# Down products of fourteen experts as two 64-row halves in two banks each, in a cross-attention and mixture-of-experts kernel

## The chip, the core and the metric

The kernel runs on one core of one Trainium2 chip. The metric is the device time of one execution in microseconds (us). Engines are called PE (TensorE; PEld is its weight load), ACT (ScalarE), DVE (VectorE), POOL (GpSimd) and SP (SyncE).

## What is computed

The reference normalizes x (8 sequences of 512 tokens, 256 wide), adds a cross-attention with 16 heads and sigmoid scores over 1601 context rows, normalizes again, and adds a feed-forward part: one shared expert over all 4096 tokens, and 16 routed experts. Every expert takes the 64 tokens of each sequence with its highest scores (8 x 64 = 512 rows) and adds its weighted output to their rows:

```python
g = einsum('becd,efd->becf', x_tok, Wg)
u = einsum('becd,efd->becf', x_tok, Wu)
h = gelu(g) * u                                  # 512 rows x 512 per expert
eo = einsum('becf,edf->becd', h, Wd) * topk_w    # the down product, 512 rows x 256
flat = flat.at[flat_idx].add(eo.reshape(-1, d))
```

## The kernel before, in words

**Numbers.** Every operand of a large product is split in two parts, hi (rounded to the fp32r format) and lo (the rest), and a product is three: hi x hi, lo x hi and hi x lo (`PRODUCTS`), summed in PSUM.

**The attention part**, up to about 893 us of the profile, works in row halves in most places: PE multiplies rows 0 to 63 and rows 64 to 127 of an operand by two matmuls that follow each other, each into a bank of its own (`ROW_TILES`, lines 1566 to 1619), and DVE adds the two banks when it reads them. The scores (line 1751) use 48 rows in each half. The weighted sum (line 1780) uses 128 rows with 32 columns of the array for each of four matmuls. The first tasks (`BEFORE`, lines 1669 and 1682, and `out_product`, line 1634, for the last sequence) do the same products with whole 128-row matmuls.

**The expert part** is a loop over 24 units: the shared expert on the 8 sequences (n = 0 to 7), then the 16 experts (n = 8 to 23, e = n - 8, so n = 9 is the second expert). A unit has four quarters of the hidden width: PE makes the gate and the up product of a quarter (`up`, line 1839, 6 matmuls of 128 x 128 by 512 columns for each), ACT takes the gelu of the gate (`gelus`, line 891), DVE multiplies it by the up product (`hidden_products`, line 1321), ACT writes the hi part of the result (`hidden_hi`, line 899) and DVE the lo part (`hidden_lo`, line 1328). PE's order in `expert(e)` is written out by hand: quarters 0 and 1 of unit n, the down product of unit n - 1, quarters 2 and 3 of unit n. The last unit, n = 23, is cut finer and has a down product of its own (`last_down`).

**The down product** (`down`, line 1857) makes four tiles of 128 rows x 256. Each is 3 products x 4 quarters = 12 matmuls with 128 x 128 weights (the hidden rows) and 256 moving columns (the down weights). Tiles 0 and 1 lie in the one bank of `d_bank` (the third `score` pair), tiles 2 and 3 in the other; `d_full` counts the filled banks. The banks `acc` and `misc` are used for transposed tokens of the first two experts and for the last unit's tiles, and are idle between.

**After it** ACT scales each tile by the token weights into `result` (`expert_result`, line 944), which it may start when DVE has written `add_w` (`expert_rows`, line 1364), and counts `scaled` after every second tile. POOL waits for `scaled` and adds the rows to the output in HBM by indirect DMA (`add_rows`, line 814). PE waits for `scaled` before it writes a bank again. DVE's order in `expert(e)` is: hidden quarters 0 and 1 of unit n, the next expert's tokens (line 1402 to 1404), a transpose (line 1392), the lo part of the next gate and up weights (line 1341), `expert_rows(e - 1)`, hidden quarters 2 and 3 (lines 1321 and 1328), the lo part of the next down weights. ACT's order is: gelus and hi parts of quarters 0 and 1, the hi part of the next gate and up weights, `expert_result(e - 1)`, quarters 2 and 3.

Of the kernel before, what the change touches and what calls it, by code (L numbers as in the profile page):

```python
# [10 lines left out]
ACT = mybir.ActivationFunctionType  # L11
AX_X = mybir.AxisListType.X

P = 128
B, S, D = 8, 512, 256
# [4 lines left out]
TT = S // P  # L20
# [28 lines left out]
FT = F // P  # L49
SETS = E + 1  # L50
UNITS = B + E
# [5 lines left out]
def key_rows(st):  # L57

    return min(P, T - P * st)
# [166 lines left out]
    return i % FT, slice(S // 2 * (i // FT), S // 2 * (i // FT + 1))  # L226


def wait_past(engine, sem, value):

    if value > 0:
        engine.wait_ge(sem, value)


def build(nc, x, ctx_t, w_attn, gate_t, w_gu, w_d, out):


    with ExitStack() as keep:
        def sem(name):
            return keep.enter_context(nc.semaphore(name))  # L240
# [59 lines left out]
        add_w = [sb(f"add_w{p}", [P, TT]) for p in range(2)]  # L300
# [26 lines left out]
        with ExitStack() as stage_b:  # L327
# [16 lines left out]
            d_hi = [d_hi0, sb("d_hi1", [P, FT, D], F32R)]  # L344
            d_lo = [d_lo0, sb("d_lo1", [P, FT, D], F32R)]
# [3 lines left out]
            hid_hi = [sb(f"hid_hi{i}", [P, FT, S], F32R) for i in range(2)]  # L349
            hid_lo = [sb(f"hid_lo{i}", [P, FT, S], F32R) for i in range(2)]  # L350
            result = [sb(f"result{i}", [P, TT, D]) for i in range(2)]
# [11 lines left out]
        acc = keep.enter_context(nc.psum_tensor("acc", [P, S], F32))  # L363
        misc = keep.enter_context(nc.psum_tensor("misc", [P, S], F32))
# [14 lines left out]

        g_bank, u_bank, d_bank, t_bank = score[0], score[1], score[2], [acc, misc]  # L380

        last_bank = [d_bank[:, 0, 0:D], d_bank[:, 1, 0:D], acc[:, 0:D], misc[:, 0:D]]


# [45 lines left out]
        resid_read = [sem(f"resid_read{i}") for i in range(2)]  # L430
        g_full = sem("g_full")
        u_full = sem("u_full")
        gelu_done = sem("gelu_done")
        hidden_done = sem("hidden_done")
        hid_hi_done = sem("hid_hi_done")
# [3 lines left out]
        scaled = sem("scaled")  # L439
# [18 lines left out]
        PRODUCTS = ((0, 0), (0, 1), (1, 0))  # L458
# [369 lines left out]
        def _(act):  # L828
# [11 lines left out]
            for t in range(2):  # L840
                last = act.activation(xn[:, t, :], xn[:, t, :], ACT.Identity, bias=rs_mean[:, t:t + 1],
                                      scale=rs[:, t:t + 1])
# [24 lines left out]
            for n in range(QUADS):  # L867
                rows = key_rows(n % NST)
# [66 lines left out]
            def expert_result(e, par, tiles=range(TT)):  # L935
                act.wait_ge(adds_ready, 2 * e + 1)
                for t in tiles:
                    if e + 1 == E:
                        act.wait_ge(d_full, 2 * (e + B) + t + 1)
                        act.activation(result[par][:, t, :], last_bank[t], ACT.Copy, scale=add_w[par][:, t:t + 1]  # L940
                                       ).then_inc(scaled, 1)
                        continue
                    act.wait_ge(d_full, 2 * (e + B) + t // 2 + 1)
                    last = act.activation(result[par][:, t, :], d_bank[:, t // 2, D * (t % 2):D * (t % 2 + 1)],  # L944
                                          ACT.Copy, scale=add_w[par][:, t:t + 1])
                    if t % 2:
                        last.then_inc(scaled, 1)
# [25 lines left out]
        def _(dve):  # L973
# [236 lines left out]
            def copy_out(task):  # L1210
# [21 lines left out]
                if kind in "KV" and LAST_OF[b, task[3] if kind == "K" else task[2]] == task:  # L1232
# [6 lines left out]
                    elif kc == 2 and b + 1 < B:  # L1239
# [22 lines left out]
                                     op0=ALU.mult, op1=ALU.mult).then_inc(ln_first, 1)  # L1262
            for t in range(2, TT):
                last = dve.tensor_scalar(xn[:, t, :], xn[:, t, :], mv[:, t, 0:1], rs[:, t:t + 1],
                                         ALU.subtract, ALU.mult)
# [42 lines left out]
            def hidden_products(n, quarters):  # L1308
                for f in quarters:
                    now = FT * n + f + 1  # L1310
                    _, cols = piece(n, f)
                    of = u_bank[:, f % 2, cols]
                    if n == 0 and f < UPS_EARLY:
                        dve.wait_ge(misc_copied, COUNT["U", B - 1, 1, f])
                        of = early_up[:, 1, S * f:S * (f + 1)]
                    else:
                        dve.wait_ge(u_full, full_of(n) + f + 1)
                    dve.wait_ge(gelu_done, now)
                    wait_past(dve, hid_split, now - 2)

                    dve.tensor_tensor(hidden[:, f % 2, cols], gelu[:, f % 2, cols], of,  # L1321
                                      ALU.mult).then_inc(hidden_done, 1)

            def hidden_lo(n, par, quarters):
                for f in quarters:
                    dve.wait_ge(hid_hi_done, FT * n + f + 1)
                    of, cols = piece(n, f)
                    dve.tensor_tensor(hid_lo[par][:, of, cols], hidden[:, f % 2, cols],
                                      hid_hi[par][:, of, cols].bitcast(F32), ALU.subtract
                                      ).then_inc(hid_split, 1)  # L1330

            def hidden_quarters(n, par, quarters):
                hidden_products(n, quarters)
                hidden_lo(n, par, quarters)
# [24 lines left out]
            def expert_rows(e, par):  # L1359

                dve.wait_ge(shared_out[par], SHARED_OUT)
                for t in range(TT):
                    wait_past(dve, added[t], 16 * (e - 1))
                dve.tensor_copy(add_w[par][:], slot_w[:, :, e]  # L1364
                                ).then_inc(adds_ready, 1)
                dve.tensor_copy(add_row[par][:], slot_row[:, :, e]
                                ).then_inc(adds_ready, 1)

            def rows_of(e, par, before):

                if before:

                    dve.wait_ge(rows_in[par], 8 * TT * (e - par))
                dve.tensor_copy(gather_row[par][:], slot_row[:, :, e]  # L1374
                                ).then_inc(rows_ready, 1)
# [11 lines left out]
            def turn(e):  # L1387

                par = e % 2
                dve.wait_ge(rows_in[par], 8 * TT * (e - par) + 16 * TT)  # L1390
                wait_past(dve, placed, PLACE_DMAS * (e - DIRECT_ROWS))
                dve.transpose(blocks.rearrange("p j (t q) -> p t j q", q=TURN),
                              gathered[par][:].rearrange("p t (j q) -> p t j q", q=TURN)).then_inc(turned, 1)
# [102 lines left out]
            for n in range(2, B):  # L1496
                par = n % 2
# [28 lines left out]
            def expert(e, par):  # L1526
                n = e + B
                hidden_quarters(n, par, (0, 1))
                if e + 1 < DIRECT_ROWS:
                    tokens(1 - par)  # L1530
                    rows_of(e + 3, 1 - par, True)
                elif e + 1 < E:
                    turned_tokens(e + 1)
                if e + 2 < E:
                    turn(e + 2)
                if e + 4 < E:
                    rows_of(e + 4, par, True)
                if e + 1 < E:
                    set_lo(0, par, e + 2)
                if e == 0:  # L1540
                    shared_result(B - 1)
                else:
                    expert_rows(e - 1, 1 - par)
                hidden_quarters(n, par, (2, 3))
                if e + 1 < E:
                    set_lo(1, par, e + 2)
# [9 lines left out]
        def _(pe):  # L1556
            ROW_TILES = [slice(ROWS * e, ROWS * (e + 1)) for e in range(2)]
# [288 lines left out]
            def down(n, par, slot):  # L1846

                pe.wait_ge(hid_split, FT * (n + 1))
                for t2 in range(2):
                    if n <= B:  # L1850
                        wait_past(pe, d_copied, 2 * n + t2 - 1)
                    else:
                        pe.wait_ge(scaled, 2 * (n - B) + t2 - 1)
                    for t in range(2 * t2, 2 * t2 + 2):
                        for j, (a, b) in enumerate(PRODUCTS):
                            for f in range(FT):
                                mm = pe.matmul(d_bank[:, t2, D * (t % 2):D * (t % 2 + 1)],  # L1857
                                               (hid_hi, hid_lo)[a][par][:, f, P * t:P * (t + 1)],
                                               (d_hi, d_lo)[b][slot][:, f, :],
                                               start=(j == 0 and f == 0), stop=(j == 2 and f == FT - 1))  # L1860
                    mm.then_inc(d_full, 1)
# [35 lines left out]
            for n in range(2, B):  # L1897
                par = n % 2
# [4 lines left out]
                if n == 4:  # L1903
                    pe.wait_ge(soft_step, SOFT_DONE)
                    for t in range(TT):
                        mm = pe.transpose(t_bank[0][:, P * t:P * (t + 1)],
                                          logits[:, t, :, :].rearrange("p b e -> p (b e)"), ident[:])
                    mm.then_inc(tok_full, tf.up())
                down(n - 1, 1 - par, 0)
                if n == 2:  # L1910
                    pe.wait_ge(gates_in, 16 * TT * B)
                    for t in range(TT):
                        mm = pe.transpose(t_bank[0][:, P * t:P * (t + 1)], logits_t[:, P * t:P * (t + 1)], ident[:])
# [75 lines left out]
```

## Time and profile before

| | us |
|---|---|
| median of 3 runs (lowest, highest) | 1309.55 (1308.88, 1310.62) |
| the profiled execution | 1305.85 |
| its span | 1304.0 |
| PE busy, share of the span | 98% |
| DVE, ACT, POOL busy | 56%, 76%, 22% |

The profile is of one execution. Its chain is the work that ended last, followed back step by step to what released it. The timeline lists instructions in order of time: start in us, us, engine, line, operation, output<-inputs, for PE the rows x columns of the weights and of the moving operand, and the number of merged instructions. Matmuls overlap each other, so the cost of one is read from start to start, and the second number of a row includes the tail that overlaps the next row. In brackets stands the idle time before the instruction and what ended it.

### The profile page before, as it was taken

The page shows a single profiled execution, that of the slowest core. Times are in us where ns is not written, and L with a number is a line of the kernel's source. Part 1 is how long each engine was busy: PE and PEld are TensorE (multiplying, and loading weights), DVE is VectorE, ACT ScalarE, POOL GpSimd, SP SyncE. Part 2 cuts the span into 40 slices and gives each one's busy share as a digit, 9 for nine tenths or more (in the row PEclk, how much of TensorE's full clock was granted, in tenths as well). Part 3 has the DMA queues.
Part 4 walks back from the last instruction along what each step waited for, and adds up shares of the span by engine and source line. Part 5 has one row for each costly group of instructions (what it writes and reads, how often), then busy time and mean ns, then how long its engine had stood idle before and what let it go on. Part 6 is the DMA issues. An engine that isn't in the chain of part 4 may idle for free.

```text
span 1304.0 us, 25503 instructions
## 1 busy us (share of the span) xinstructions
PE 1283.8 (98%) x10200; PEld 772.1 (59%) x10200; DVE 732.5 (56%) x1377; ACT 985.3 (76%) x1148; POOL 286.9 (22%) x288
## 2 busy tenths in 40 slices
PE   8999999999999999999999999999999999999997
PEld 6445444444454544544444443336888888888887
DVE  6564475365266448437536633215558777777773
ACT  5888989998998899899999989996333455555553
POOL 3000030020002003002000200500001567677635
PEclk9999999999999999999999999999999999999999
DMA  7785973874776597387477549713543577777754
GB/s 215 179 188 126 139 184 111 125 162 133 130 139 166 118 137 171 113 131 148 149 129 140 127 93 156 169 34 114 195 130 110 181 201 192 188 192 190 192 109 49
DMA packets 118726, 190.82 MB, mean 146 GB/s; under 512 B 22448, under 2 KB 71600, under 8 KB 118608
## 3 DMA queue, kind: packets, MB, share of 16 engines
q1 hardware_dynamic: 98768, 155.21, 51.9%
q0 software_dynamic: 19648, 33.72, 12.4%
q8 instruction: 81, 1.33, 0.5%
q10 hardware_dynamic: 192, 0.26, 0.1%
q14 instruction: 37, 0.30, 0.1%
HBM read 108.43 MB, written 55.61 MB: 126 GB/s over the span
## 4 chain that ended last, share of the span: by engine, by line
PE 87%; issue 5%; DMA 2%; DVE 2%; ACT 2%; POOL 1%; SPq 0%; POOLq 0%; DVEq 0%; ACTq 0%
PE score L1839 19%; PE score L1751 18%; PE acc L1780 14%; PE misc L1780 13%; PE score L1857 9%; PE score L1566 5%; PE score L1580 5%; PE score L1589 2%; ACT probs L876 1%; PE score L1619 1%; PE score L1607 1%; DMA key_scr<-key_parts 1%; POOL norm L765 1%; DMA norm<-norm_blocks 1%; DMA ctx_raw<-ctx_t 1%
## 5 line engine op out<-in xcount | busy, mean ns | idle before, releaser
L876 ACT ACTIVATE probs<-score 128x1024 f32<-128x1024 f32 (+1 forms) x832 | 789.8, 1026 | 77.3 <-PE score L1751 70.6
L1751 PE MATMUL score<-queries,keys 48*128 48x512 f32 (+1 forms) x1664 | 312.2, 438 | 6.5 <-ACT probs L876 4.2
L1751 PEld LDWEIGHTS score<-queries,keys 48*128 48x128 f32 (+1 forms) x1664 | 139.1, 180 | 275.0 <-ACT probs L876 212.7
L1780 PE MATMUL acc<-probs,values 128*32 128x512 f32 (+1 forms) x1664 | 210.5, 601 | 0.0
L1780 PE MATMUL misc<-probs,values 128*32 128x512 f32 (+1 forms) x1664 | 205.8, 600 | 0.0
L1026 DVE TENSOR_REDUCE whole<-score 128x512 f32<-128x1024 f32 (+1 forms) x75 | 77.0, 1026 | 196.6 <-PE score L1566 119.6
L729 POOL DMA_DIRECT2D ctx_raw<-ctx_t x32 | 23.4, 733 | 642.6 <-DVE ctx_lo L1004 557.9
L801 POOL DMA_INDIRECT gathered<-norm_scr,gather_row x64 | 81.2, 1269 | 227.5 <-DVE gather_row L1374 212.2
L891 ACT ACTIVATE gelu<-score 128x512 f32<-128x512 f32 (+1 forms) x97 | 55.5, 580 | 84.6 <-PE score L1839 84.0
L814 POOL DMA_INDIRECT out<-result,add_row x64 | 106.6, 1666 | 48.4 <-ACT result L944 25.9
L1839 PE MATMUL score<-tok_hi,gu_hi 128*128 128x512 f32 (+1 forms) x388 | 117.0, 383 | 0.0
L1839 PE MATMUL score<-tok_lo,gu_hi 128*128 128x512 f32 (+1 forms) x388 | 116.2, 381 | 0.0
L1839 PE MATMUL score<-tok_hi,gu_lo 128*128 128x512 f32 (+1 forms) x388 | 116.2, 381 | 0.0
L1321 DVE TENSOR_TENSOR hidden<-gelu,score 128x512 f32<-128x512 f32 (+1 forms) x97 | 64.0, 664 | 92.6 <-PE score L1839 62.3
L899 ACT ACTIVATE hid_hi<-hidden 128x512 fp32r<-128x512 f32 (+1 forms) x100 | 61.0, 613 | 63.9 <-DVE hidden L1321 60.7
L1066 DVE TENSOR_REDUCE values<-score 128x512 f32<-128x1024 f32 (+1 forms) x52 | 59.3, 1141 | 71.7 <-PE score L1580 71.0
L1780 PEld LDWEIGHTS misc<-probs,values 128*32 128x32 f32 (+1 forms) x1664 | 40.7, 108 | 87.0 <-issue 76.6
L1780 PEld LDWEIGHTS acc<-probs,values 128*32 128x32 f32 (+1 forms) x1664 | 38.8, 108 | 77.0 <-issue 71.5
L1839 PEld LDWEIGHTS score<-tok_lo,gu_hi 128*128 128x128 f32 x388 | 71.8, 188 | 14.2
L1839 PEld LDWEIGHTS score<-tok_hi,gu_lo 128*128 128x128 f32 x388 | 71.8, 188 | 14.1
L1839 PEld LDWEIGHTS score<-tok_hi,gu_hi 128*128 128x128 f32 x388 | 70.2, 189 | 12.9 <-issue 0.8
L944 ACT ACTIVATE result<-score,add_w 128x256 f32<-128x256 f32 x60 | 23.6, 474 | 67.9 <-DVE add_w L1364 64.7
(257 smaller groups left out, 1626.2 us busy)
## 6 DMA issues: line engine op xcount, KB each, us to landing
keys<-key_scr SPq DMA_DIRECT2D x180, 200.2 KB, 8.0
key_scr<-key_parts SPq DMA_DIRECT2D x45, 512.0 KB, 8.3
gu_raw<-w_gu SPq DMA_DIRECT2D x17, 1024.0 KB
ctx_raw<-ctx_t POOLq DMA_DIRECT2D x24, 512.0 KB, 5.1
queries<-query_parts SPq DMA_DIRECT2D x186, 64.0 KB, 2.5
d_raw<-w_d SPq DMA_DIRECT2D x17, 512.0 KB
norm<-xn SPq DMA_DIRECT2D x224, 32.0 KB
xn<-x SPq DMA_DIRECT2D x8, 512.0 KB, 3.8
```

The lines of the kernel that those rows point to most:

```text
L801: pool.indirect_dma_start(gathered[par][:, t, :], None, norm_scr[:, :], bass.IndirectOffsetOnAxis(ap=gather_row[par][:, t:t + 1], axis=0)) ...
L814: pool.indirect_dma_start(out[:, :], bass.IndirectOffsetOnAxis(ap=add_row[par][:, t:t + 1], axis=0), result[par][:, t, :], None, compute_o ...
L876: act.activation(probs[0:rows, (n + 1) % RING, 2 * pair:2 * pair + 2, :], score[SLOT[k]][0:rows, :, :], ACT.Sigmoid, scale=SCALE).then_inc ...
L899: act.activation(hid_hi[par][:, of, cols], hidden[:, f % 2, cols], ACT.Copy).then_inc(hid_hi_done, 1)
L1026: dve.tensor_reduce(whole[:, 0:n], score[SLOT[task]][:, :, 0:n].rearrange("p e s -> p s e"), AX_X, ALU.add).then_inc(halves_added, 1)
L1321: dve.tensor_tensor(hidden[:, f % 2, cols], gelu[:, f % 2, cols], of, ALU.mult).then_inc(hidden_done, 1)
L1566: mm = pe.matmul(bank[:, e, 0:n], W2[a][rows, WK, k, P * half:P * (half + 1)], parts_of_ctx(b, kc)[c][rows, k, 0:n], start=(j == 0 and k = ...
L1580: mm = pe.matmul(bank[0:n, e, D * i:D * (i + 1)], parts_of_ctx(b, kc)[a][rows, k, s0:s0 + n], W2[c][rows, WV, k, :], start=(j == 0 and k = ...
L1751: mm = pe.matmul(score[SLOT[k]][0:rows, g, :], keys[quarter % KEY_RING][of, pair, P * st:P * st + rows], queries[half][of, e, pair, :], st ...
L1780: mm = pe.matmul(sums_bank[n // NST % 2][32 * c:32 * (c + 1), :], values[b % 2][0:rows, st, half, c, :], probs[0:rows, (n + 1) % RING, c, ...
L1839: mm = pe.matmul(bank[:, f % 2, cols], (gu_hi, gu_lo)[a][slot][:, w, k, P * of:P * (of + 1)], (tok_hi, tok_lo)[b][par][:, k, cols], start= ...
L1857: mm = pe.matmul(d_bank[:, t2, D * (t % 2):D * (t % 2 + 1)], (hid_hi, hid_lo)[a][par][:, f, P * t:P * (t + 1)], (d_hi, d_lo)[b][slot][:, f ...
```

## The change

For the units with 8 < n < 23 (the second to the fifteenth expert) the down product is cut into two: rows 0 to 63 and rows 64 to 127 of every quarter of the hidden width are multiplied by separate matmuls, which alternate, into two banks: tiles 0 and 1 into the two banks of `d_bank`, tiles 2 and 3 into `acc` and `misc`. ACT scales the first half into `result` and counts the new semaphore `half_scaled`; DVE waits for that, multiplies the other half by the same weights and adds it to `result`, and counts `scaled` after every second tile. DVE does this between `expert_rows` and hidden quarters 2 and 3. The first expert, the shared expert and the last unit stay as they were.

```diff
@@ -224,6 +224,12 @@
     if n + 1 < UNITS:
         return i, slice(0, S)
     return i % FT, slice(S // 2 * (i // FT), S // 2 * (i // FT + 1))
+
+
+def in_halves(n):
+
+
+    return B < n < UNITS - 1
 
 
 def wait_past(engine, sem, value):
@@ -378,6 +384,8 @@
                         o_lo[:]]
 
         g_bank, u_bank, d_bank, t_bank = score[0], score[1], score[2], [acc, misc]
+
+        down_halves = [[d_bank[:, 0, :], d_bank[:, 1, :]], [acc[:], misc[:]]]
 
         last_bank = [d_bank[:, 0, 0:D], d_bank[:, 1, 0:D], acc[:, 0:D], misc[:, 0:D]]
 
@@ -430,6 +438,7 @@
         resid_read = [sem(f"resid_read{i}") for i in range(2)]
         g_full = sem("g_full")
         u_full = sem("u_full")
+        half_scaled = sem("half_scaled")
         gelu_done = sem("gelu_done")
         hidden_done = sem("hidden_done")
         hid_hi_done = sem("hid_hi_done")
@@ -941,6 +950,10 @@
                                        ).then_inc(scaled, 1)
                         continue
                     act.wait_ge(d_full, 2 * (e + B) + t // 2 + 1)
+                    if in_halves(e + B):
+                        act.activation(result[par][:, t, :], down_halves[t // 2][0][:, D * (t % 2):D * (t % 2 + 1)],
+                                       ACT.Copy, scale=add_w[par][:, t:t + 1]).then_inc(half_scaled, 1)
+                        continue
                     last = act.activation(result[par][:, t, :], d_bank[:, t // 2, D * (t % 2):D * (t % 2 + 1)],
                                           ACT.Copy, scale=add_w[par][:, t:t + 1])
                     if t % 2:
@@ -1366,6 +1379,16 @@
                 dve.tensor_copy(add_row[par][:], slot_row[:, :, e]
                                 ).then_inc(adds_ready, 1)
 
+            def other_halves(e, par):
+
+                for t in range(TT):
+                    dve.wait_ge(half_scaled, TT * (e - 1) + t + 1)
+                    last = dve.scalar_tensor_tensor(
+                        out=result[par][:, t, :], in0=down_halves[t // 2][1][:, D * (t % 2):D * (t % 2 + 1)],
+                        scalar=add_w[par][:, t:t + 1], in1=result[par][:, t, :], op0=ALU.mult, op1=ALU.add)
+                    if t % 2:
+                        last.then_inc(scaled, 1)
+
             def rows_of(e, par, before):
 
                 if before:
@@ -1541,6 +1564,8 @@
                     shared_result(B - 1)
                 else:
                     expert_rows(e - 1, 1 - par)
+                    if in_halves(n - 1):
+                        other_halves(e - 1, 1 - par)
                 hidden_quarters(n, par, (2, 3))
                 if e + 1 < E:
                     set_lo(1, par, e + 2)
@@ -1852,7 +1877,14 @@
                     else:
                         pe.wait_ge(scaled, 2 * (n - B) + t2 - 1)
                     for t in range(2 * t2, 2 * t2 + 2):
-                        for j, (a, b) in enumerate(PRODUCTS):
+                        for j, (a, b) in enumerate(PRODUCTS if in_halves(n) else ()):
+                            for f in range(FT):
+                                for e, rows in enumerate(ROW_TILES):
+                                    mm = pe.matmul(down_halves[t2][e][:, D * (t % 2):D * (t % 2 + 1)],
+                                                   (hid_hi, hid_lo)[a][par][rows, f, P * t:P * (t + 1)],
+                                                   (d_hi, d_lo)[b][slot][rows, f, :],
+                                                   start=(j == 0 and f == 0), stop=(j == 2 and f == FT - 1))
+                        for j, (a, b) in enumerate(() if in_halves(n) else PRODUCTS):
                             for f in range(FT):
                                 mm = pe.matmul(d_bank[:, t2, D * (t % 2):D * (t % 2 + 1)],
                                                (hid_hi, hid_lo)[a][par][:, f, P * t:P * (t + 1)],
```

## Rows read from the trace of the kernel before

**Rows 1.** page, its first line:

```profile
span 1304.0 us, 25503 instructions
```

**Rows 2.** the chain of waits in order of time: start us, us, what:

```profile
1062.75 5.75 PE score L1857 x48
...
1085.16 10.91 PE score L1839 x48
...
1276.76 5.76 PE score L1857 x48
```

**Rows 3.** windows: stretch, us, busy by engine (instructions), PEclk, DMA share, GB/s:

```profile
1100.00:1268.00 168.00, 168.00 (x974) 149.07 (x973) 123.17 (x180) 88.55 (x140) 108.75 (x72) 1.00 0.77 180
```

**Rows 4.** timeline of PE, blocks of whole and of half matmuls, and what follows them:

```profile
15.08 0.40 PE L1682 MATMUL score<-w_lo,ctx_hi 128*128 128x256 f32 x2
...
17.59 0.62 PE L1669 MATMUL misc<-ctx_hi,w_hi 128*128 128x512 f32 x2
...
366.33 0.40 PE L1607 MATMUL score<-w_hi,o_hi 64*128 64x256 f32 x4
...
367.75 0.63 PE L1751 MATMUL score<-queries,keys 48*128 48x512 f32 x4
...
378.15 0.39 PE L1580 MATMUL score<-w_hi,ctx_lo 64*128 64x256 f32 x4
...
379.06 0.88 PE L1751 MATMUL score<-queries,keys 48*128 48x512 f32 x4
...
896.37 0.40 PE L1634 MATMUL misc<-w_hi,o_hi 128*128 128x256 f32 x2
...
897.80 0.63 PE L1839 MATMUL score<-tok_hi,gu_hi 128*128 128x512 f32 x2
```

**Rows 5.** timeline of PE, first step from 128-row matmuls to row halves:

```profile
24.18 0.63 PE L1669 MATMUL misc<-ctx_next,w_lo 128*128 128x512 f32 x2
24.74 0.74 PE L1751 MATMUL score<-queries,keys 48*128 48x512 f32 x4
25.31 0.64 PE L1566 MATMUL score<-ctx_hi,w_hi 64*128 64x512 f32 x4
```

**Rows 6.** timeline of PE, row halves, 128 x 32 matmuls, row halves:

```profile
36.28 0.40 PE L1751 MATMUL score<-queries,keys 48*128 48x512 f32 x2
36.61 1.06 PE L1780 MATMUL acc<-probs,values 128*32 128x512 f32 x8
37.61 0.74 PE L1751 MATMUL score<-queries,keys 48*128 48x512 f32 x4
38.17 0.64 PE L1566 MATMUL score<-ctx_hi,w_hi 64*128 64x512 f32 x4
38.63 0.65 PE L1566 MATMUL score<-ctx_lo,w_hi 64*128 64x512 f32 x4
...
41.82 1.92 PE L1780 MATMUL acc<-probs,values 128*32 128x512 f32 x16
43.67 0.72 PE L1751 MATMUL score<-queries,keys 48*128 48x512 f32 x4
```

**Rows 7.** timeline of DVE and ACT behind the down product that ends at 1085.16:

```profile
1086.98 0.16 DVE L1364 COPY add_w<-slot_w 128x4 f32<-128x4 f32 x1
...
1087.17 1.57 ACT L944 ACTIVATE result<-score,add_w 128x256 f32<-128x256 f32 x4 [4.57 <-DVE add_w L1364]
...
1089.32 0.69 DVE L1321 TENSOR_TENSOR hidden<-gelu,score 128x512 f32<-128x512 f32 x1 [2.10 <-issue]
1090.67 0.69 DVE L1321 TENSOR_TENSOR hidden<-gelu,score 128x512 f32<-128x512 f32 x1 [0.66 <-PE score L1839]
1091.27 1.50 DVE L1328 TENSOR_TENSOR hid_lo<-hidden,hid_hi 128x512 fp32r<-128x512 f32 x2
```

**Rows 8.** groups of instructions by form: xcount, busy us, mean ns, idle before:

```profile
L1135 DVE SCALAR_TENSOR_TENSOR o_sum<-misc,mine,o_sum 128x512 f32<-128x512 f32 x16 | 12.0, 749 | 32.6 <-PE misc L1780 32.6
...
L1173 DVE TENSOR_TENSOR nt_lo<-score,nt_hi 128x256 fp32r<-128x256 f32 x28 | 10.6, 420 | 0.5
```

## The prediction, made before the changed kernel had run

> **What bounds the kernel now.** I read the page first, for the span [rows 1], then the chain of waits in order of time over the part that the change touches. The first of the fourteen changed down products starts there at 1062.75 us and the last at 1276.76 us; between them the chain is PE alone, and it repeats: a down product of 48 matmuls takes 5.75 us, and the 48 matmuls of the gate and up products behind it take 10.91 us, with nothing between them [rows 2]. One expert is 16.66 us long. The windows view says the same from the other side: in 168 us of this stretch PE is busy for 168.00, at a granted clock of 1.00 (the 2.4 GHz level), while VectorE is busy for 123, ScalarE for 89 and GpSimd for 109 [rows 3]. So whatever PE gains or loses in a down product goes one for one into the time, and what is added on VectorE costs nothing as long as it makes PE wait for nothing.
>
> **PE: the matmuls themselves.** The 48 matmuls of 128 rows by 256 columns become 96 of 64 rows by 256 columns. Now one takes 5.75 / 48 = 119.8 ns from start to start [rows 2]. If the two halves ran one after the other, it would be twice that. The attention part already issues such pairs, and in it they run side by side. The best comparison is the output projection, since it exists in both forms with the same operands (o_hi, o_lo and the projection's weights, 256 columns): whole, 12 matmuls from 896.37 to 897.80 us are 119.2 ns each; in halves, 24 from 366.33 to 367.75 us are 59.2 ns each, 118.3 ns for a pair [rows 4]. A second comparison is the value product: whole, 22 matmuls from 15.08 to 17.59 us are 114.1 ns each; in halves, 16 from 378.15 to 379.06 us are 56.9 ns each, 113.8 ns for a pair [rows 4]. The pace follows the operands, not the form. I therefore put the pair at what the whole matmul costs now and the sum of this term at 0. Its bounds: the down pairs reach the value product's 113.8 ns, 48 x 6.0 ns = 0.29 us per expert, -4.0 us over fourteen; or they lose as the 512-column halves do, where 4 matmuls from 38.17 to 38.63 us are 230 ns for a pair [rows 6] against 10.91 / 48 = 227 ns for a whole one [rows 2], 48 x 3 ns = 0.14 us per expert, +2.0 us.
>
> **PE: the change of form.** Before and after each changed product PE now goes from matmuls on all 128 rows to matmuls on 64 rows and back. The part touched has no such step today, since gate, up and down all use 128 rows, but the attention part has. Where it first goes from 128-row matmuls to row halves, the last two whole matmuls take 0.56 us to the next start instead of 2 x 0.227 = 0.45, and the first four halves 0.57 us instead of 0.46 [rows 5, 6]: 0.22 us for one step. The way back to 128 x 128 doesn't stand alone in the trace. What does is the round trip between row halves and the 128 x 32 matmuls of the weighted sum: the two halves ahead of it take 0.33 us against 0.23, the eight narrow matmuls 1.00 us against 0.85 (sixteen take 1.85, so eight more are 0.85), the four halves behind it 0.56 us against 0.46 [rows 6]. That is 0.10 + 0.15 + 0.10 = 0.35 us for a round trip. One down product has one round trip. Twice the first number would be 0.44, and if only the stretched start after each step is real it is 2 x 0.10 = 0.20 us. I take 0.35 us, the one complete round trip: 14 x 0.35 = +4.9 us, with 14 x 0.20 = 2.8 and 14 x 0.44 = 6.2 as ends.
>
> The Trainium skill, page "TensorEngine Tiling (Array Packing)", Key Properties, says that a change of the tiling mode (not of the tile) drains TensorE. It speaks against this change, and the stretched groups above agree with it.
>
> **VectorE and ScalarE.** ScalarE issues the same four scalings of 256 columns per expert as before, on banks that fill at the same points of the down product; its cost is 0. VectorE gets four operations of 128 x 256 that read one PSUM bank and the scaled half. None such is in the trace; a subtraction of 256 columns out of PSUM takes 0.42 us, and the same kind of operation on 512 columns 0.75 us [rows 8]. I put one at 0.45, nearer the first as it has the same width, with 0.42 and 0.75 as ends: 1.8 us per expert, so that VectorE is busy for about 14 of 16.66 us.
>
> They lie here. Take the down product that ends at 1085.16 us, where the next gate product starts [rows 2]. There ScalarE starts its four scalings only at 1087.17, because it waits for add_w, which VectorE writes at 1086.98 behind its other work [rows 7]. The first scaling ends about 0.47 us later (1.57 us for four overlapping ones), at 1087.64, and the four additions then run until 1087.64 + 4 x 0.45 = 1089.44 us. Queued behind them on VectorE is the hidden product of the third quarter, which starts at 1089.32 now: 0.12 us late. Behind it is the hidden product of the fourth quarter at 1090.67, which waits for PE's up product and so starts as before, and with it the low parts at 1091.27 [rows 7]. At 0.75 us each the additions end at 1090.64, the third quarter's product at 1091.33, and PE asks for it only for the next expert's first up product, one gate product of six matmuls (1.36 us) after 1090.61, at 1091.97. The low parts would then end at 1093.4 instead of 1092.77, and the next down product starts at 1096.07. So this costs 0 at both ends, covered by PE's own third and fourth quarters; without that cover it would be 1.8 us per expert, 25 us. GpSimd's scattered additions wait for the result half a microsecond longer, but first run the four gathers of a later expert, so they start no later. SP's queue gets and loses nothing. PE's waits for freed banks name counts that are reached an expert earlier; nothing queues behind them. The banks acc and misc are free by then, as only the first two experts' tokens pass through them. The tail after the last expert isn't touched.
>
> **Sum.** 0 + 4.9 + 0 = +4.9 us. The profiled execution took 1305.85 us (span 1304.0 us [rows 1] and 1.85 around it), the median of the runs is 1309.55, 0.3% above. Added to the profiled execution it is 1310.75; added to the median, which is what is compared, 1314.5 us, +0.37%. A measurement of this kernel can tell about 0.2% from no change, 2.6 us, so 1306.9 to 1312.2 counts as the same.
>
> **Rivals.**
> (a) The step between the forms is cheap, or its price is partly given back by a quicker pair: 14 x 0.20 = 2.8 us at an unchanged pace, down to 2.8 - 4.0 = -1.2. Speaking for it: the two sides of my step estimate may count the same lost time, once as a late start and once as a stretched group, and the value product shows that 114 ns is possible. Against it: the comparison of both forms with the same operands. About 1308.4 to 1312.4, middle 1311. Chance 0.27.
> (b) It gets faster: a 64-row weight load slips under a matmul that runs on the other 64 rows, so that the gap per matmul goes. 256 columns at the 2.4 GHz that the granted clock of 1.00 stands for are 106.7 ns, so 13.1 ns of the 119.8 are such a gap; 48 x 13.1 = 0.63 us per expert, -8.8 us in all, +4.9 for the steps: 1305.7 us. It decides from the point where a pair falls below 119.8 - 4.9 / (14 x 48) us = 112.5 ns. No pair in the attention part stays below that, so I give it 0.10.
> The Trainium skill has this as a rule, on the page "TensorE: Matmul & The Clock Gate", Part 3, "The mechanism": weight loads overlap matmuls in flight only where the row group differs, which would leave the whole matmuls their gap and take it from the halves. The equal pace of both forms in [rows 4] speaks against its counting here.
> (c) The additions become the wait: if VectorE is done with them later than about 1091.3 us in the expert above (over 0.9 us each with the hand-over from ScalarE), the third quarter's product is late for PE's up product. At 1.2 us each it would be 1087.64 + 4.8 + 0.69 = 1093.1 against 1091.97, 1.1 us per expert, some +16 on top: 1330 us. Nothing of this width takes that long in the trace; chance 0.04.
> (d) The halves don't run side by side, so the change doesn't do what it says: 48 x 119.8 ns = 5.75 us more per expert, +80 us, 1390 us. All halves of the attention part speak against it; 0.02.
>
> **How the numbers follow.** My forecast, steps at 0.25 to 0.44 us per expert and the pace unchanged or slightly worse, has 0.57 and gives 1314.5, by itself 1312.4 to 1317.8 (6.2 + 2.0 on top of the median at the upper end). The range takes in (a) down to 1309.5 and, for steps dearer between 128 x 128 and halves than in the attention part, reaches to 1318.5; it leaves out (b), (c), (d) and the edge of (a). Faster by over 0.2%: (b), 0.10. Slower by over 0.2%: the forecast, (c) and (d), 0.57 + 0.04 + 0.02 = 0.63. Within: (a), 0.27.
>
> **What would show it.** In the chain of waits the down product's pieces of an expert should be 5.9 to 6.2 us (96 matmuls) with the gate and up pieces at 10.9 to 11.1, an expert of about 17.0 us. In the timeline four halves should start every 0.24 us, with the first group about 0.1 longer and the first gate product behind it as well. VectorE's four additions should take 0.42 to 0.5 us each, before the third quarter's hidden product, with PE waiting for nothing. Groups of four at 0.215 us would make (b) right; a PE idle time put down to VectorE's hidden product, (c); a steady 0.48 us, (d). I am wrong above all if the gate products behind a changed one are not stretched, since the whole loss rests on that.

## The result, and the profile after

The changed kernel takes 1314.43 us (median of 16 runs, 1311.99 to 1322.99), the kernel before in the same series 1308.98 us (16 runs, 1306.91 to 1312.06). The ratio is 1.0046, 95% interval 1.0032 to 1.0060: slower, by 5.4 us by the medians (the interval is 4.2 to 7.9 us), where 4.9 was forecast. The profiled execution took 1313.62 us, with a span of 1311.7 us and a granted clock of 0.999.

The chain of waits of the changed kernel, in order of time (start us, us, what), answers to [rows 2]. The half matmuls of tiles 2 and 3 alternate between the banks `acc` and `misc` and so are listed one by one, which is left out here:

```profile
1138.97 11.10 PE score L1864 x48
...
1150.07 3.06 PE score L1883 x48
...
1156.01 11.10 PE score L1864 x48
```

From one up product to the next are 1156.01 - 1138.97 = 17.04 us, where it was 16.66. The down product between them takes 1156.01 - 1150.07 = 5.94 us instead of 5.75, and the gate and up products 11.10 instead of 10.91: 0.19 us each, 0.38 us per expert. The windows view of the same stretch as in [rows 3] (PE, PEld, DVE, ACT, POOL busy):

```profile
1100.00:1268.00 168.00, 167.96 (x1419) 145.13 (x1417) 137.30 (x218) 87.27 (x138) 112.85 (x73) 1.00 0.76 182
```

PE is as full as before at the same granted clock; VectorE has 14.1 us more to do in 168 us and ScalarE as much as before. So the 0.38 us are spent inside PE. The timeline of PE around an earlier changed product shows where:

```profile
1080.75 0.62 PE L1864 MATMUL score<-tok_lo,gu_hi 128*128 128x512 f32 x2
1081.20 0.61 PE L1864 MATMUL score<-tok_hi,gu_lo 128*128 128x512 f32 x2
1081.75 0.74 PE L1883 MATMUL score<-d_hi,hid_hi 64*128 64x256 f32 x8
1082.32 0.64 PE L1883 MATMUL score<-d_lo,hid_hi 64*128 64x256 f32 x8
1082.80 0.64 PE L1883 MATMUL score<-d_hi,hid_lo 64*128 64x256 f32 x8
...
1087.48 0.28 PE L1883 MATMUL acc<-d_hi,hid_lo 64*128 64x256 f32 x1
1087.48 0.28 PE L1883 MATMUL misc<-d_hi,hid_lo 64*128 64x256 f32 x1
1087.68 0.73 PE L1864 MATMUL score<-tok_hi,gu_hi 128*128 128x512 f32 x2
1088.26 0.62 PE L1864 MATMUL score<-tok_lo,gu_hi 128*128 128x512 f32 x2
1088.72 0.62 PE L1864 MATMUL score<-tok_hi,gu_lo 128*128 128x512 f32 x2
```

Read from start to start. Two 512-column matmuls take 0.45 us, but the two ahead of the first halves take 0.55 (1081.20 to 1081.75). Eight halves take 0.48 us, so a pair takes 120 ns, as a whole matmul did; but the first eight take 0.57. On the way back the last pair takes 0.20 us instead of 0.12, and the first two gate matmuls 0.58 instead of 0.46. That is 0.10 + 0.09 + 0.08 + 0.12 = 0.39 us, the 0.38 within rounding, and nothing else in the expert is longer. The trace shows where the time is lost, not what PE does in it.

VectorE and ScalarE behind this down product, in the timeline, answer to [rows 7]:

```profile
1089.64 0.16 DVE L1377 COPY add_w<-slot_w 128x4 f32<-128x4 f32 x1
...
1090.35 0.88 DVE L1386 SCALAR_TENSOR_TENSOR result<-score,add_w,result 128x256 f32<-128x256 f32 x2 [0.47 <-ACT result L954]
1091.14 0.87 DVE L1386 SCALAR_TENSOR_TENSOR result<-misc,add_w,result 128x256 f32<-128x256 f32 x2
1091.99 0.69 DVE L1334 TENSOR_TENSOR hidden<-gelu,score 128x512 f32<-128x512 f32 x1
1093.46 0.69 DVE L1334 TENSOR_TENSOR hidden<-gelu,score 128x512 f32<-128x512 f32 x1 [0.78 <-issue]
```

The four additions run from 1090.35 to about 1092.0 us. The third quarter's hidden product starts right behind them, 4.3 us after the next gate product's start (1091.99 - 1087.68), as before the change (1089.32 - 1085.00; the timeline has that start at 1085.00, the chain of waits at 1085.16). The fourth quarter's starts after 0.78 us of idle time, so the additions hold up nothing behind it.

The two profiled spans differ by 7.7 us, more than the medians. 1.7 us of that lie ahead of the first changed product, which starts at 1064.46 instead of 1062.75 us. From there to the start of the last unit's own down product are 231.57 us (1064.46 to 1296.03) instead of 225.53 (1062.75 to 1288.28), +6.0: fourteen times 0.38 are 5.3, and two down products have a single stall of 0.3 us each.

### The profile page after: what moved, and what is told of

Its sections match the earlier page's. It is cut to its first block and busy times, and to the rows that moved or that the text cites. A ratio compares the mean times of both kernels' runs of the same rounds, so it can differ in the third digit from the quotient of the medians.

```text
span 1311.7 us, 26903 instructions
## 1 busy us (share of the span) xinstructions
PE 1291.2 (98%) x10872; PEld 772.2 (59%) x10872; DVE 757.4 (58%) x1433; ACT 985.4 (75%) x1148; POOL 290.0 (22%) x288
## 5 line engine op out<-in xcount | busy, mean ns | idle before, releaser
L823 POOL DMA_INDIRECT out<-result,add_row x64 | 109.7, 1714 | 47.6 <-DVE result L1386 25.5
L1341 DVE TENSOR_TENSOR hid_lo<-hidden,hid_hi 128x512 fp32r<-128x512 f32 (+1 forms) x100 | 65.8, 668 | 4.9 <-ACT hid_hi L908 0.2
```

Source lines behind the costliest of these rows:

```text
L823: pool.indirect_dma_start(out[:, :], bass.IndirectOffsetOnAxis(ap=add_row[par][:, t:t + 1], axis=0), result[par][:, t, :], None, compute_o ...
```

## The experiments

The theory is that every change of PE between 128-row and 64-row matmuls costs 0.19 us, that pairs of halves cost what whole matmuls cost, and that the additions are covered. Each ratio is to runs of the kernel before on the same chip and in the same series; it isn't the quotient of the two medians beside it, from which it differs by up to 0.0016. There are three series on three chips, in which the kernel before has medians of 1309.23, 1306.62 and 1306.52 us. The shortest period of an expert, read from the timeline, is given beside it, since it is free of stalls that come and go between executions.

**Whole matmuls, but two banks and the additions.** Quarters 0 and 1 go into one bank, 2 and 3 into the other:

```diff
 for f in range(FT):
-    for e, rows in enumerate(ROW_TILES):
-        mm = pe.matmul(down_halves[t2][e][...], hid[par][rows, f, ...], d[slot][rows, f, :], ...)
+    mm = pe.matmul(down_halves[t2][f // 2][...], hid[par][:, f, ...], d[slot][:, f, :], ...)
```

> The down products stay 128-row matmuls, but quarters 0 and 1 go into one bank and quarters 2 and 3 into the other, with the same scaling and the same added VectorE operations as in the change. Theory (the loss is PE's change between 128-row and 64-row form, 0.19 us each way): no step of form, so ratio 1.000 to the kernel before, 16.66 us per expert. Rival (the loss is VectorE's additions or the two more banks): ratio 1.004, 17.04 us per expert.

Measured: 1309.5 us (12 runs) against 1309.23, ratio 0.9986, interval 0.9959 to 1.0013. Its down products take 5.75 us, and of the thirteen gate and up pieces of full length around them seven take 10.90 or 10.91 us, so the period is 16.66 us where nothing stalls. In the other six PE stalls by 0.05 to 1.0 us, 3.1 us in all, and three of these stalls end with ScalarE's third gelu. The loss of 0.38 us in every expert goes with the halves, not with the banks or the additions. The interval leaves room for 1.7 us of cost, no more. Whether the two banks and the additions make such stalls more frequent isn't shown: none of the three profiles with the old down product has a stall among the fourteen experts, and the profiles with two banks have between none and these 3.1 us.

**Halves, but no additions.** ScalarE's scaling counts `scaled` itself and VectorE adds nothing, so half of each changed product is missing in the output:

```diff
-    if in_halves(n - 1):
-        other_halves(e - 1, 1 - par)
```

> Halves as in the change, but VectorE's additions are left out, so that the second half of every changed product is missing in the output. Theory: ratio 1.004, 17.04 us per expert as in the change, with VectorE back at its old work. Rival (VectorE's additions): ratio 1.000.

Measured: 1313.87 us (12 runs) against 1309.23, ratio 1.0024, interval 0.9996 to 1.0052, +4.6 us by the medians. The interval alone doesn't decide, but the trace does: 17.04 us in ten experts (5.94 and 11.10), with VectorE's work back at 119.87 us in the 168 us stretch. Taking the additions away gives nothing back.

**Tiles 0 and 1 in halves, tiles 2 and 3 whole**, and **tiles 0 and 2 in halves, tiles 1 and 3 whole.** Both have 48 half matmuls per expert instead of 96. VectorE works on all four tiles as before; where there is nothing to add it multiplies by one:

```diff
-for j, (a, b) in enumerate(PRODUCTS if in_halves(n) else ()):
+for j, (a, b) in enumerate(PRODUCTS if in_halves(n) and t < 2 else ()):        # or t % 2 == 0
 ...
-for j, (a, b) in enumerate(() if in_halves(n) else PRODUCTS):
+for j, (a, b) in enumerate(() if in_halves(n) and t < 2 else PRODUCTS):        # or t % 2 == 0
```

> Only tiles 0 and 1 of a changed product in halves, tiles 2 and 3 whole: half as many half matmuls, but still one round trip between the forms per expert. Theory: 0.38 us per expert as in the change, ratio 1.004. Rival (every half matmul costs a little, 5.3 us / 1344 = 4 ns each): 0.19 us per expert, ratio 1.002.

> Tiles 0 and 2 in halves, tiles 1 and 3 whole: as many half matmuls as with two tiles, but two round trips per expert. Theory: 2 x 0.38 = 0.76 us per expert, +10.6 us, ratio 1.008. Rival (a price per half matmul): 0.19 us per expert, ratio 1.002.

Measured: two tiles 1313.29 us (12 runs), ratio 1.0020, interval 0.9996 to 1.0045; alternating 1317.54 us (12 runs), ratio 1.0054, interval 1.0032 to 1.0077; before 1309.23. By the medians +4.1 and +8.3 us. The chain of waits with two tiles in halves, in an expert with 0.13 us of other stalls:

```profile
1138.33 11.04 PE score L1867 x48
1149.37 3.06 PE score L1886 x48
1152.42 3.06 PE acc L1892 x24
1155.49 10.91 PE score L1867 x48
```

and its timeline of PE at the step back, now inside the down product:

```profile
1134.62 0.64 PE L1886 MATMUL score<-d_hi,hid_lo 64*128 64x256 f32 x8
1135.19 0.74 PE L1892 MATMUL acc<-d_hi,hid_hi 128*128 128x256 f32 x4
1135.77 0.64 PE L1892 MATMUL acc<-d_lo,hid_hi 128*128 128x256 f32 x4
1136.24 0.64 PE L1892 MATMUL acc<-d_hi,hid_lo 128*128 128x256 f32 x4
...
1138.16 0.63 PE L1867 MATMUL score<-tok_hi,gu_hi 128*128 128x512 f32 x2
1138.63 0.62 PE L1867 MATMUL score<-tok_lo,gu_hi 128*128 128x512 f32 x2
```

The last eight halves and the first four whole matmuls take 0.57 and 0.58 us instead of 0.48, and the gate product behind the whole tiles is no longer stretched (0.47 to the next start). The stretch has moved with the step. The usual period is 6.03 + 11.00 = 17.03 us, the same as with 96 halves. In the alternating kernel it is 6.39 + 11.00 = 17.39 us with as few halves and two round trips: +0.73 against +0.37. So the cost follows the number of steps and not the number of halves, and one step is 0.18 to 0.19 us. The measured ratios are at the edge of or below what was expected (1.004 and 1.008): by the trace the fourteen experts cost 5.2 and 10.2 us, by the medians 4.1 and 8.3. What the shortfall of 1 to 2 us is stays open. The kernel before stands 2.6 us higher in this series than in the two others; if that were waits of its own that the other kernels share in part, it would explain it, but no profile of the kernel before was taken in this series.

**Seven experts only.**

```diff
-    return B < n < UNITS - 1
+    return B < n <= B + 7
```

> The change for the seven experts n = 9 to 15 alone. Theory (one round trip between the forms per changed product): seven experts of 17.04 us and seven of 16.66 us, +2.7 us, ratio 1.002. Rival (a cost that comes once, with the longer program): the whole +5.4 us, or nothing.

Measured: 1309.12 us (12 runs) against 1306.62, ratio 1.0014, interval 0.9989 to 1.0038, +2.5 us by the medians. The timeline has 17.04 us from the second to the seventh changed expert and 16.66 us behind them. The cost comes anew with each changed product.

**The same halves in another order.** Of each tile first the twelve on rows 0 to 63, then the twelve on rows 64 to 127:

```diff
-for j, (a, b) in enumerate(PRODUCTS):
-    for f in range(FT):
-        for e, rows in enumerate(ROW_TILES):
+for e, rows in enumerate(ROW_TILES):
+    for j, (a, b) in enumerate(PRODUCTS):
+        for f in range(FT):
```

> The same 96 half matmuls per changed product, but of each tile first the 12 on rows 0 to 63 and then the 12 on rows 64 to 127. Theory that two halves run side by side only when neighbours alternate between the rows: 5.75 us more per expert, +80 us. Rival (PE pairs them whatever the order): as the change, 1314 us.

Measured: 1354.74 us in one run against 1306.62, +48 us. Neither expectation holds: a down product takes 9.02 us, +3.08 over the alternating order instead of +5.75. Its timeline of PE:

```profile
1105.05 0.64 PE L1883 MATMUL score<-d_lo,hid_hi 64*128 64x256 f32 x4
1105.53 0.28 PE L1883 MATMUL score<-d_hi,hid_lo 64*128 64x256 f32 x1
1105.54 0.38 PE L1883 MATMUL score<-d_hi,hid_hi 64*128 64x256 f32 x1
1105.65 0.28 PE L1883 MATMUL score<-d_hi,hid_lo 64*128 64x256 f32 x1
1105.76 0.28 PE L1883 MATMUL score<-d_hi,hid_hi 64*128 64x256 f32 x1
1105.77 0.28 PE L1883 MATMUL score<-d_hi,hid_lo 64*128 64x256 f32 x1
1105.88 0.28 PE L1883 MATMUL score<-d_hi,hid_hi 64*128 64x256 f32 x1
1105.89 0.28 PE L1883 MATMUL score<-d_hi,hid_lo 64*128 64x256 f32 x1
1105.99 0.28 PE L1883 MATMUL score<-d_hi,hid_hi 64*128 64x256 f32 x1
1106.11 0.64 PE L1883 MATMUL score<-d_lo,hid_hi 64*128 64x256 f32 x4
```

Four halves on the same rows take 0.48 us, 120 ns each, as much as a whole matmul. Around the border between two blocks the last four halves of one (d_hi, hid_lo) run beside the first four of the next (d_hi, hid_hi), which by the records start ahead of halves that were issued before them. These eight take 0.58 us (1105.53 to 1106.11) instead of 8 x 0.12 = 0.96. Seven borders in a down product save 2.7 us of the 96 x 0.12 = 11.5, and with 0.2 for the steps that is the measured 9.02. So the side-by-side execution is what makes the changed form as fast as the old one, and across a border PE finds it for four pairs by itself.

**The kernel before again.**

> The kernel before, unchanged, for a second profile of it. Theory: an expert is 16.66 us wherever PE doesn't wait; the waits of some 3 us in all that lie between the shown profile (1305.85 us) and the median (1309 us) are single stalls of up to 1 us in which PE waits for ScalarE's third gelu, and they belong to both kernels. Rival: they belong to the additions of the changed kernel alone, and none is seen here.

Measured: 1316.28 us in this single execution, at a granted clock of 0.995. All the same its experts are 16.66 us, and its gelus come as regularly as in the first profile. The theory fell: no stall was seen among the experts. That is what the rival said would be seen, but it doesn't make the additions the cause, since the halves without additions have a stall of 0.26 us. The time over the other profile was lost ahead of the experts, since the down product that started at 1045.93 us there starts at 1056.32 us here. 3.3 of these 10.4 us were lost by 816 us. The other 7.1 us begin on VectorE. Its rows and GpSimd's in the first profile:

```profile
816.05 1.38 DVE L1117 TENSOR_SCALAR norm<-resid,mv,rs 128x256 f32<-128x256 f32 x4
817.37 1.89 POOL L784 CAST gu_hi<-gu_raw 128x2048 fp32r<-128x2048 f32 x1 [91.59 <-DMA d_raw<-w_d]
```

and in this one, with PE's row behind them:

```profile
819.38 10.27 DVE L1117 TENSOR_SCALAR norm<-resid,mv,rs 128x256 f32<-128x256 f32 x4
819.44 1.89 POOL L784 CAST gu_hi<-gu_raw 128x2048 fp32r<-128x2048 f32 x1 [92.03 <-DMA d_raw<-w_d]
851.62 1.22 PE L1751 MATMUL score<-queries,keys 48*128 48x512 f32 x4 [5.11 <-DVE early_up L1182]
```

The four operations of line 1117 take 10.27 us instead of 1.38 where GpSimd's conversion of the weights starts 0.06 us after the first of them instead of at their end. PE then waits for 5.11 us, and in the stretch from 850 to 855 us the granted clock is 0.53, which is the 1.2 GHz level for most of it. Of the thirteen profiles two more have the same, with 8.0 and 8.6 us for the four operations and waits of PE of 2.56 and 4.89 us: seven experts only, and add_w written first in the changed kernel. In the profile of the change they take 2.96 us and no gap of PE follows; in the nine others they take 1.38. No run moved GpSimd's work, so that GpSimd is the cause is read from the traces and not tested. It isn't the change that brings it, since this is the kernel before.

**add_w written first, in the kernel before.**

```diff
+if e:
+    expert_rows(e - 1, 1 - par)
 if e + 1 < E:
     set_lo(0, par, e + 2)
 if e == 0:
     shared_result(B - 1)
-else:
-    expert_rows(e - 1, 1 - par)
```

> The kernel before, with VectorE writing add_w and add_row ahead of the low part of the next gate and up weights, so that ScalarE can scale the down product right after it ends and its third gelu is no longer late. Theory of the stalls above: they go, ratio 0.998 (about 1306 us). Rival (PE doesn't depend on it): 1.000.

Measured: 1306.76 us (11 runs) against 1306.62, ratio 1.0001, interval 0.9985 to 1.0017. The third gelu does come earlier, but PE has no use for it. My theory of the stalls isn't borne out: there was nothing to gain in this series, and no version that beats the kernel before was found.

**add_w written first, in the changed kernel**, with the additions left behind the long subtraction.

> The change, with VectorE writing add_w and add_row ahead of its long subtraction, so that ScalarE's scalings and the additions can start about 2 us earlier. Theory (the additions lie under PE's third and fourth quarters in any case): an expert stays at 17.04 us, ratio to the kernel before 1.004. Rival (a part of the loss is the late end of the additions): below 1.003.

Measured: 1311.68 us (7 runs) against 1306.52, ratio 1.0040, interval 1.0027 to 1.0052, +5.2 us, with 17.04 us per expert (5.93 and 11.11). Earlier scalings change nothing.

**The additions twice, and three times**, the extra ones into spare tiles that nothing reads:

```diff
+for spare in (o_hi, o_lo)[0:1]:          # [0:2] for three times
+    dve.scalar_tensor_tensor(out=spare[...], in0=down_halves[t // 2][1][...], scalar=add_w[par][:, t:t + 1],
+                             in1=result[par][:, t, :], op0=ALU.mult, op1=ALU.add)
```

> The change with each of VectorE's four additions issued once more into a spare tile, 1.75 us more VectorE work per expert. By the profile of the change the third quarter's hidden product then ends about 6.7 us after the down product, and PE asks for it 6.9 us after it. Theory: still covered, 17.04 us per expert, at most 0.2 us more. Rival (the cover is already gone): 17.04 + 1.75 us, +24 us in all.

> The same with two more additions each, 3.5 us more VectorE work per expert. Theory: VectorE needs 12.1 + 3 x 1.9 = 17.8 us per expert, more than PE's 17.04, and PE waits for the third quarter's hidden product: an expert of 17.8 to 18.7 us, +11 to +23 us over the change. Rival (PE never depends on it): 17.04 us.

Measured: twice 1312.08 us (4 runs), ratio 1.0031, interval 1.0008 to 1.0055, with 17.04 us per expert; three times 1327.27 us (2 runs), ratio 1.0156, interval 1.0136 to 1.0176, with 12.20 + 5.93 = 18.1 us per expert. So the cover takes four more additions and not eight. With three times, the chain of waits leaves PE:

```profile
1145.08 2.19 DVE gu_lo L1354
...
1147.76 1.19 ACT result L954 x3
1148.96 0.50 ACT gelu L900
...
1149.95 0.39 DVEq L238
1150.34 0.39 DVE o_hi L1387
...
1151.52 0.39 DVE o_hi L1387
...
1152.69 0.60 DVE hidden L1334
...
1153.34 2.83 PE score L1868 x11
```

PE's up product of the next expert's first quarter starts right behind the third quarter's hidden product, which is the wait of rival (c), at the place where it was put. Its size fits too: rival (c) put 1.1 us per expert on an addition of 1.2 us, and three that follow each other at 0.39 us (1.18 in all) cost 18.1 - 17.04 = 1.1.

## Why the prediction was right, point by point

**What bounds the kernel.** PE alone, through all fourteen experts. The 14.1 us more of VectorE's work in 168 us cost nothing, and 0.19 us more in each of two PE pieces came through in full.

**The matmuls themselves.** Put at 0, with bounds of -4.0 and +2.0 us. Eight halves take 0.48 us, four whole ones took 0.48: 120 ns per pair and 119.8 ns per whole matmul. Comparing both forms with the same operands [rows 4] gave the right answer, where taking the value product's 114 ns for the pairs would have been 4 us off.

**The change of form.** Put at 0.35 us for a round trip, measured 0.38: 5.3 us instead of 4.9 for fourteen. The measured 5.4 can't confirm the sum to that, since its interval goes from 4.2 to 7.9; the period of the experts does. Taken from another round trip, row halves to 128 x 32 and back, it was 0.03 too low; twice the one step from 128-row matmuls to halves [rows 5] would have been 0.44, 0.06 too high. That the two round trips cost nearly the same was partly luck: no row of the kernel before had the step back to 128 x 128, and the trip that was used has its parts elsewhere (0.10 + 0.15 + 0.10 against 0.10 + 0.09 + 0.08 + 0.12). Moving the steps moved the stretched groups, and doubling them doubled the cost. The stretch on both sides of a step, which rival (a) took for one loss counted twice, is real on both sides: 0.10 ahead and 0.09 behind the step into halves.

**VectorE.** One addition was put at 0.45 us. It is 0.48 us long and 0.39 to 0.40 from start to start, so all four took 1.6 instead of 1.8 us, and the third quarter's hidden product isn't late at all where 0.12 us were expected. The cover was worked out as ending when an addition takes 0.9 us; two of 0.39 behind each other are still covered and three are not, which agrees. GpSimd's work is in its place, and nothing waits for it.

**The rivals.** (a) fell with the step's price of 0.38 us. (b) fell with the pace of 120 ns per pair; no pair of the changed products is quicker. The rule of the Trainium skill behind it ("TensorE: Matmul & The Clock Gate", Part 3, "The mechanism"), that weight loads overlap matmuls in flight only where the row groups differ, isn't borne out here: a pair takes 120 ns and a whole matmul 119.8. By the records the weight loads of whole matmuls overlap matmuls too, since in [rows 3] they are busy for 149.07 us of 168 in which PE's matmuls never stop. The 13.1 ns over the 106.7 stay in both forms, and what they are stays open. (c) was shown to be the next wait: four further additions per expert are still covered, eight are not. (d) fell too, but only because the halves alternate: in blocks by row they take 14 x 3.08 = 43 us more than alternating, and the rest of the 80 us that were worked out for halves one after the other is hidden at the borders.

## What to carry to other kernels

A product that filled all 128 rows gained nothing here from being cut into row halves: a pair that runs side by side takes what one whole matmul takes, and among whole neighbours each cut product pays for two changes of form, 0.38 us. The halves must also alternate between the rows in the order of issue. Price such a change by counting the steps between forms, not the matmuls, and look up the price in groups around an existing step, ahead of it and behind it. Where the same product exists in both forms in one trace, it answers what an average over other products doesn't.

## What had not been expected

Halves issued in blocks by row still overlap around the border of two blocks, four on each side: 96 of them took 9.02 us, where 96 x 120 ns are 11.5.

Three profiled executions were 5 to 10 us longer than the medians of their kernels. In these three, and in none of the ten others, four normalizing operations of VectorE took 8.0 to 10.3 us while GpSimd was at work, with a wait of PE of 2.6 to 5.1 us and a lower granted clock behind it.

In several profiles ScalarE and VectorE start late behind PE's products: later than PE's own records end, with the idle time put down to PE. In the changed kernel ScalarE's gelu of the second quarter starts between 1.25 us ahead of the down product's first matmul and 0.7 us behind it, from one expert to the next; in both profiles of the kernel before it is 1.16 us ahead in all experts but the last of these, whose products are cut finer. It isn't tied to the additions, since the kernel without them shows it too (from 1.25 ahead to 0.36 behind), nor to the halves alone, since seven experts in halves don't show it and the whole form with two banks does. It mostly costs no time, but the stalls of up to 1 us in the whole form with two banks come after such late starts. What delays them stays open.
